# Layer 1 of a two-layer model: the last 52 of 128 slot scatters made in the experts' stage, row loads that wait by expert

## The chip, the cores and the metric

The kernel runs on one core of a Trainium2 chip. The metric is the time of one execution on the device in microseconds (us), lower is better. Before the change three runs took 2988.72, 2998.57 and 2993.95 us, median 2993.95. Engines: PE (TensorE), DVE (VectorE), ACT (ScalarE), POOL (GpSimd) and SP (SyncE), which mostly issues DMAs. DMAs issued by SP go over queue q1, those of ACT over q10, those of POOL (the indirect ones) over q0. They share 16 DMA engines.

## The reference

x is (4, 512, 512) in float32, 2048 tokens of 512 numbers. Four steps are added to it one after the other: a state-space layer, a first mixture of experts, a cross attention and a second mixture of experts. The change touches only the second mixture ("layer 1"):

```python
scores = sigmoid(x @ router_w)                      # 2048 tokens x 32 experts
# the best 4 of 8 groups of experts, then the best 8 experts of those (with a bias)
tkw = 2.5 * scores[chosen] / sum(scores[chosen])
xs = repeat(x, 8)[sort by expert]                   # 16384 rows, sorted by expert
down = (silu(xs @ w_gate[e]) * (xs @ w_up[e])) @ w_down[e]
routed = sum over a token's 8 rows of down * tkw
out = x + routed + silu(x @ sw_gate) * (x @ sw_up) @ sw_down     # x normalised in each
```

Each expert has w_gate and w_up of 512 x 256 and w_down of 256 x 512.

## The kernel before

Each stage is a block with a program for every engine; a barrier of all engines stands between two stages. Two stages make up layer 1.

**The routing stage** (`route_stage` with L = 1). DVE normalises the tokens into the tile `xn` (r_xn in the trace), PE and ACT make the logits, and DVE picks 8 experts for each token. Every expert gets a run of slots in the DRAM tensor `slots_in1`, in half tiles of 64 slots. A token's 8 slots stand in `scat`, the largest first (DVE's MAX8 gives them in falling order), so k = 7 is the slot of its lowest expert. POOL then copies the rows into their slots with 128 indirect DMAs (line 882, "scatters"): one for each of 16 tiles of 128 tokens and each k. Four semaphores `written` count them in turn. In the first half scatter n waits until n-2 has landed, in the second half until n-4 has. Beside this PE computes the shared expert (lines 1218 and 1237), and DVE adds it to x (line 1046). SP loads the weights of the first three experts and stores x to the output. The stage ends with waits for all 128 scatters and for all stores.

**The experts' stage** (`expert_stage1`). It walks over 144 tiles of 128 slots. ACT loads the rows in groups of four tiles into a ring of two groups (line 1933 the rows in four pieces, 1938 and 1940 the weights and token numbers), and reloads a ring place while the tiles pass (`reload`, called in turn t). For each tile PE does gate and up (2092), turns the hidden rows (2101) and does down (2114), in the order turn(t-1), up(t), down(t-1). DVE transposes rows (2009), copies the turned hidden rows (2014), multiplies (2019), finds each row's weight and address (`addressed`, 2038 to 2045) and copies half of w_down (2027). ACT makes silu (1921), scales the result into one of `OUT` = 8 result tiles `yo` (1928), and copies half of the gate and up weights (1947). POOL adds each result tile to the output with two indirect DMAs of 64 rows (1874, "adds"), so there are 288 of them. SP refills the weights of an expert when `down` of the last tile of an earlier one is done.

The ring of eight result tiles ties POOL to the others. `added` is raised when POOL starts the adds of tile t (from t = 2 on), which means that tile t-2 has landed. Before the address and the result of tile t are written, for t from 8 on, DVE (`addressed`) and ACT (`empty`) wait until tile t-8 has landed, that is until POOL starts the adds of tile t-6. In DVE's order `addressed(t)` stands ahead of the copy of the weights for tile t+1 and of the hidden rows of tile t.

Of the kernel before, what the change touches and what calls it, by code (L numbers as in the profile page):

```python
# [48 lines left out]
AHEAD = RING1 - 1  # L49
XW = H + 32  # L50
# [28 lines left out]
class Pools:  # L79
# [15 lines left out]
    def sem0(self, name):  # L95
        self.from0.append(self.sem(name))
        return self.from0[-1]

# [597 lines left out]

def route_stage(nc, c, I, D, x, L, route, ahead=None, out=None):
# [10 lines left out]
    with ExitStack() as ctx:  # L708
# [7 lines left out]
        if L == 0:  # L716
            xn, xnT = route["xn"], route["xnT"]
        else:
            xn = sb("xn", [P, NT, XW])
            xnT = sb("xnT", [P, B, KH, S])  # L720
# [60 lines left out]
        NARROW = NT * K if L == 0 else NT * K // 2  # L781
        written = [pl.sem0(R + f"written{lane}") for lane in range(LANES)]
# [6 lines left out]
        with nc.Block() as block:  # L789

            @block.sync
            def _(sp):
# [46 lines left out]
                else:  # L839
                    for a in range(2):  # L840
                        sp.dma_start(out[T + a * P:T + (a + 1) * P, :].rearrange("p (a z) -> p a z", z=P),
                                     bc(c["zeros"][:, :], 1, H // P)).then_inc(sem["xout"], 16)
# [4 lines left out]
                    for b in range(B):  # L847
                        sp.wait_ge(sem["xadd"], 1 + TB * (b + 1))
                        sp.dma_start(out[b * S:(b + 1) * S, :].rearrange("(t p) h -> p t h", p=P),
                                     x[:, b * TB:(b + 1) * TB, :]).then_inc(sem["xout"], 16)  # L850
                    sp.wait_ge(sem["eidout"], 1 + 16)
                    sp.wait_ge(sem["ahead"], 1 + 48 * AHEAD)
                    sp.wait_ge(sem["xout"], 1 + 16 * (B + 2))

            @block.gpsimd
            def _(pool):
# [14 lines left out]
                for t in range(NT):  # L871
                    if L == 1 and t < TB:
                        pool.wait_ge(sem["idx0"], 1 + t + 1)
                    else:
                        pool.wait_ge(sem["idx"], 1 + t // TB + 1 - L)
                    for k in range(K):
                        n = t * K + k
                        lane = n % LANES
                        ahead_of = n - 2 if n < NARROW else n - LANES
                        if ahead_of >= 0:  # L880
                            pool.wait_ge(written[ahead_of % LANES], 16 * (ahead_of // LANES + 1))
                        pool.indirect_dma_start(slots[:, :], bass.IndirectOffsetOnAxis(scat[:, t, k:k + 1], 0),  # L882
                                                xn[:, t, 0:XU], None, bounds_check=nslot - 1, oob_is_err=False)\
                            .then_inc(written[lane], 16)
                for lane in range(LANES):
                    pool.wait_ge(written[lane], 16 * NT * K // LANES)
# [52 lines left out]
            def _(dve):  # L939
# [188 lines left out]
                if L == 1:  # L1128
# [8 lines left out]
                    dve.tensor_copy(tei[:, :], te[:, :]).then_inc(sem["eid"], 1)  # L1137
                if L == 0:
# [640 lines left out]
def expert_stage1(nc, c, I, D, x, ends, W, out):  # L1779
# [3 lines left out]
    with ExitStack() as ctx:  # L1783
# [4 lines left out]
        OUT = 2 * RING  # L1788
        assert E % RING == 0
        assert AHEAD == RING - 1  # L1790
        wgu, wd = W["wgu"], W["wd"]
        assert OUT == 2 * RING
# [47 lines left out]
        with nc.Block() as block:  # L1840

            @block.sync
            def _(sp):
# [22 lines left out]
            def _(pool):  # L1866
# [3 lines left out]
                pool.iota(within_i[:, :], [[32, NTILE1 // 2], [0, 2]], base=0, channel_multiplier=0).then_inc(sem["iota"], 1)  # L1870
                pool.wait_ge(sem["after"], 1 + 2)
# [45 lines left out]
            def _(act):  # L1917
# [31 lines left out]

                def reload(t, q):  # L1950
                    place = q % RING
                    if place == RING - 2:
                        hold(act, sem["xsT"], 1 + t + 2, c["held"])
                        load_rows((t + RING + 2) * P, q // RING, (0, 1))
                    if place == RING - 1:
                        load_rows((t + RING + 1) * P, q // RING, (2,))
                    if place == 0:
                        load_rows((t + RING) * P, 1 - q // RING, (3,))
                    if place == 1:
                        hold(act, sem["dest"], 1 + t - 1, c["held"])  # L1960
                        load_rec((t + RING - 1) * P, 1 - q // RING)
# [29 lines left out]
                for q in range(REST):  # L1991
                    t = (TURNS - 1) * OUT + q
                    gate(t, q)
                    if q < 2:
                        reload(t, q)
# [6 lines left out]
            def _(dve):  # L2002
# [27 lines left out]
                def addressed(t, q, n):  # L2030
                    row = rec[:, q // RING, q % RING, :]
                    word = token[:, q // RING, q % RING * 2:q % RING * 2 + 2, 0]
                    if q % RING == 0:
                        dve.wait_ge(rec_in[q // RING], 32 * n)
# [13 lines left out]
                def a_round(i, first=False, last=False):  # L2048
                    for q in range(REST if last else OUT):
                        t = i * OUT + q  # L2050
                        if not (last and q == REST - 1):
                            turned_rows(t + 1, q + 1, i + (q + 1) // OUT + 1)
# [3 lines left out]
                        addressed(t, q, i + 1)  # L2056
# [1067 lines left out]
def program(nc, I, out, upto=9):  # L3124
    with ExitStack() as ctx:
# [34 lines left out]
        if upto >= 5:  # L3160
            route1 = {"ln": ln1, "wr": wr1, "bias": bias1, "scat": pl.sb("scat1", [P, NT, K1], I32), "ends": pl.sb("ends", [1, 1 + E], I32)}
            W = {"wgu": pl.sb("e1_wgu", [P, RING1, KH, 2 * F1]), "wd": pl.sb("e1_wd", [P, RING1, F1 // P, H])}
            route_stage(nc, c, I, D, x, 1, route1, W, out)
        if upto >= 6:
            expert_stage1(nc, c, I, D, x, route1["ends"], W, out)
# [52 lines left out]
```

## Time and profile before

| | |
|---|---|
| median of three runs | 2993.95 us |
| the profiled execution | 2994.6 us |
| its span in the profile | 2992.8 us |
| PE busy | 2622.1 us (88%) |
| DVE busy | 1535.3 us (51%) |
| ACT busy | 1032.8 us (35%) |
| POOL busy | 1294.2 us (43%) |

How to read it: a share is that of the whole span, over stages with different limits. Layer 1 lies in the last third. The chain that ended last is followed back from the last instruction. In a timeline row the number in square brackets is how long the engine stood idle before the instruction, and the name behind the arrow is what ended this; "issue" means nothing that the profile shows.

### The profile page before, as it was taken

Reading aid. Unit: us, or ns where it says so; the run is one execution under the profiler, and the core shown is the slowest. Engines: PE = TensorE matmul, PEld = TensorE weight load, DVE = VectorE, ACT = ScalarE, POOL = GpSimd, SP = SyncE. Lnnn points to the kernel's source line nnn. Section 1 sums busy time; section 2 is a strip of 40 time slices with the busy share of each in tenths; the row PEclk is TensorE's granted clock in tenths of the full one; section 3 lists DMA queues with packets and bytes.
Section 4 is the critical chain, followed back from the end, with each engine's and each line's share of the span. In section 5 each row is a group of like instructions: output and inputs, shape, how many; then the busy total and the mean of one; then the engine's idle time right before and its main releaser. Section 6 shows DMA issues by size and latency. Waiting matters only on the chain. (4 is left out here: it accounts for less than half of the span.)

```text
span 2992.8 us, 41291 instructions
## 1 busy us (share of the span) xinstructions
PE 2622.1 (88%) x11315; PEld 1086.1 (36%) x11318; DVE 1535.3 (51%) x2654; ACT 1032.8 (35%) x1305; POOL 1294.2 (43%) x933
## 2 busy tenths in 40 slices
PE   5888976699999987768999999798099999999998
PEld 1343432244444433323333333443033333333333
DVE  7999999631110032136666564731045555555554
ACT  4646564120000011023443333200055555555553
POOL 2767656312300032116565633146535455545554
PEclk8999999999999999889999999899599999999999
DMA  3433222310210289982067100254657776787764
GB/s 127 116 96 105 86 64 71 123 50 22 86 33 14 80 283 353 287 216 82 1 175 195 42 1 1 73 217 187 207 137 158 160 155 121 139 219 158 161 119 61
DMA packets 361887, 372.82 MB, mean 125 GB/s; under 512 B 85810, under 2 KB 268403, under 8 KB 361778
## 3 DMA queue, kind: packets, MB, share of 16 engines
q1 hardware_dynamic: 202210, 239.03, 25.4%
q0 software_dynamic: 45520, 93.26, 14.7%
q10 hardware_dynamic: 114048, 39.16, 5.9%
q8 instruction: 58, 0.95, 0.1%
q14 instruction: 51, 0.42, 0.1%
HBM read 231.96 MB, written 152.14 MB: 128 GB/s over the span
## 5 line engine op out<-in xcount | busy, mean ns | idle before, releaser
L1874 POOL DMA_INDIRECT out_x<-e_yo,e_dest x288 | 418.7, 1454 | 411.0 <-DMA out_x<-e_yo,e_dest 281.4
L2092 PE MATMUL e_psg<-e_wgu,e_xsT 128*64 x1152 | 519.9, 594 | 83.0 <-ACT e_cgu L1947 83.0
L2092 PE MATMUL e_psg<-e_cgu,e_xsT 128*64 128x512 f32 x1152 | 519.9, 594 | 0.0
L287 POOL TENSOR_TENSOR hc<-hs,bcst 128x1024 f32<-128x1024 f32 x128 | 300.8, 2350 | 179.6 <-DVE ps_b L507 170.6
L1947 ACT ACTIVATE e_cgu<-e_wgu 128x2048 f32 x144 | 275.1, 1911 | 133.0 <-issue 130.6
L632 PE MATMUL ps_y<-hc,ident 128*128 128x512 f32 x512 | 241.2, 609 | 89.4 <-POOL hc L287 89.2
L513 DVE TENSOR_TENSOR_SCAN hs<-dA,ps_b 128x1024 f32<-128x1024 f32 x128 | 292.7, 2286 | 8.1 <-ACT dA L417 3.9
L2092 PEld LDWEIGHTS e_psg<-e_wgu,e_xsT 128*64 128x64 f32 x1152 | 154.2, 137 | 332.0 <-issue 332.0
L2114 PE MATMUL e_pso<-e_wd,e_hT 128*64 x576 | 270.7, 592 | 0.7 <-DVE e_hT L2014 0.7
L2114 PE MATMUL e_pso<-e_cd,e_hT 128*64 128x512 f32 x576 | 270.7, 592 | 0.0
L1237 PE MATMUL r_ps_t<-r_wd,r_h 128*128 128x512 f32 x480 | 210.7, 600 | 9.6 <-DVE r_h L984 5.1
L917 ACT ACTIVATE r_sg<-r_ps_g 128x512 f32<-128x512 f32 x60 | 35.8, 597 | 525.2 <-PE r_ps_g L1218 493.8
L984 DVE TENSOR_TENSOR r_h<-r_ps_u,r_sg 128x512 f32<-128x512 f32 x60 | 41.4, 692 | 319.3 <-PE r_ps_u L1218 289.8
L417 ACT ACTIVATE dA<-dt,a_neg 128x511 f32<-128x511 f32 x256 | 165.2, 713 | 102.4 <-DVE hs L513 97.4
L2702 DVE TENSOR_REDUCE a_nm<-a_ps 128x2 f32<-128x992 f32 x128 | 146.1, 1185 | 89.5 <-PE a_ps L2946 89.1
L2019 DVE TENSOR_TENSOR e_h<-e_psg,e_sg 128x256 f32<-128x256 f32 x144 | 61.2, 425 | 254.0 <-ACT e_sg L1921 232.2
L2464 ACT ACTIVATE a_pt<-a_ps 128x1024 f32<-128x1024 f32 (+1 forms) x128 | 126.2, 1022 | 181.0 <-PE a_ps L2963 120.2
L882 POOL DMA_INDIRECT slots_in<-r_xn,scat x128 | 126.3, 987 | 133.9 <-DMA slots_in<-r_xn,scat 54.6
L632 PEld LDWEIGHTS ps_y<-hc,ident 128*128 128x128 f32 x512 | 92.8, 191 | 232.4 <-POOL hc L287 138.5
L2009 DVE STREAM_TRANSPOSE e_xsT<-e_xs 128x512 f32<-128x512 f32 x144 | 168.4, 1169 | 5.5 <-DMA e_xs<-slots_in 5.5
L1928 ACT ACTIVATE e_yo<-e_pso,e_wrow 128x512 f32<-128x512 f32 x144 | 99.1, 688 | 207.7 <-PE e_pso L2114 178.5
L2027 DVE COPY e_cd<-e_wd 128x1024 f32 x144 | 101.9, 708 | 129.4 <-PE e_pso L2114 113.0
(426 smaller groups left out, 4202.3 us busy)
## 6 DMA issues: line engine op xcount, KB each, us to landing
slots_in<-zeros SPq DMA_DIRECT2D x144, 256.0 KB
e_xs<-slots_in ACTq DMA_DIRECT2D x144, 256.0 KB
bcst<-bc_rows SPq DMA_DIRECT2D x128, 256.0 KB, 4.2
e_wgu<-in_wg SPq DMA_DIRECT2D x32, 512.0 KB
e_wgu<-in_wu SPq DMA_DIRECT2D x32, 512.0 KB
e_wd<-in_wd SPq DMA_DIRECT2D x32, 512.0 KB
e_w<-in_wg SPq DMA_DIRECT2D x11, 1408.0 KB
e_w<-in_wu SPq DMA_DIRECT2D x11, 1408.0 KB
```

The lines of the kernel that those rows point to most:

```text
L287: pool.tensor_tensor(hc[:, it % 2, half(h), :], hs[:, it % 2, half(h), :], bc(bcst[:, q, 1, :], 1, HB), ALU.mult).then_inc(sem["hc"], 1)
L417: i = act.activation(dA[:, it % 2, t, 1:], dt[:, b % 2, t, 1:], ACT.Exp, scale=a_neg[:, n, t:t + 1])
L513: dve.tensor_tensor_scan(hs[:, it % 2, half(h), :].rearrange(flat), dA[:, it % 2, half(h), :].rearrange(flat), ps_b[:, :, :].rearrange(fla ...
L632: i = pe.matmul(ps_y[:, t, :], c["ident"][:, :], hc[:, it % 2, t, :], start=False, stop=False, skip_group_check=True)
L882: pool.indirect_dma_start(slots[:, :], bass.IndirectOffsetOnAxis(scat[:, t, k:k + 1], 0), xn[:, t, 0:XU], None, bounds_check=nslot - 1, oo ...
L1237: i = pe.matmul(ps_t[:, j % 2, :], h[:, f, j * P:(j + 1) * P], wd[:, f, :], start=f == 0, stop=f == FC - 1)
L1874: pool.indirect_dma_start(out[:, :], bass.IndirectOffsetOnAxis(dest[:, q, s:s + 1], 0), yo[half(s), q, :], None, bounds_check=T + 2 * P - ...
L1947: act.activation(cgu[:, q % 2, :, :], wgu[:, bass.ds(e % RING, 1), :, :].rearrange("p o k n -> p (o k) n"), ACT.Copy).then_inc(sem["cgu"], 1)
L2009: dve.transpose(xsT[:, q % 2, :, :].rearrange("p k (s j) -> p k s j", j=DQ), xs[:, q // RING % 2, part, :].rearrange("p s (i k) -> p k s i ...
L2092: j = pe.matmul(ps_g[half(s), q % 2, :], xsT[:, q % 2, k, half(s)], w, start=k == 0, stop=k == KH - 1, tile_position=(0, s * HALF), skip_g ...
L2114: j = pe.matmul(ps_o[half(s), q % 2, :], hT[:, q % 2, a, half(s)], w, start=a == 0, stop=a == NW - 1, tile_position=(0, s * HALF), skip_gr ...
L2702: dve.tensor_reduce(nm[:, i % 8, 2 * z:2 * z + 2], ps[:, at:at + 2, 0:S2], AX_X, ALU.max, negate=True)\
```

## The change

POOL makes 76 scatters in the routing stage and the other 52 in the experts' stage, ahead of its first add. The order is new: `SLOT_ORDER` has the 32 of tokens 0 to 511 as before, then for tokens 512 and on by rank, k = 7 of all twelve tiles of tokens, then k = 6, and so on. Every scatter now waits for n-2. The wait for all 128 and for the stores of x stands ahead of POOL's first add. The tile `xn` and the semaphores live across both stages.

ACT loads a group of rows when the scatters that can write to it have landed. DVE works this out in the routing stage for groups 0 to 3, by the experts that end ahead of the group's last half tile (ten small instructions, `rows_held`). ACT reads the number, and waits on the four semaphores. It now loads group 1 behind the first two copies of weights. SP makes its first refill of weights only when group 1 has landed. No load beyond the last group is made any more. `OUT` is 8 as before; the rest of the edits (`PER`, `% 2`, `GROUPS`) write the same numbers in a general form.

```diff
+LANES1 = 4
+SLOT_ORDER = [(t, k) for t in range(TB) for k in range(K1)] + [(t, k) for k in reversed(range(K1)) for t in range(TB, NT)]
+EARLY = 76
+GROUPS_HELD = 4
...
+def write_slots(pool, D, route, n):
+
+    t, k = SLOT_ORDER[n]
+    written = route["written"]
+    if n >= 2:
+        pool.wait_ge(written[(n - 2) % LANES1], 16 * ((n - 2) // LANES1 + 1))
+    pool.indirect_dma_start(D["xs1"][:, :], bass.IndirectOffsetOnAxis(route["scat"][:, t, k:k + 1], 0),
+                            route["xn"][:, t, 0:H + 2 * K1 + 1], None, bounds_check=NSLOT1 - 1, oob_is_err=False)\
+        .then_inc(written[n % LANES1], 16)
...
-                    sp.wait_ge(sem["xout"], 1 + 16 * (B + 2))
...
+                    for n in range(EARLY):
+                        if n < TB * K and n % K == 0:
+                            pool.wait_ge(sem["idx0"], 1 + n // K + 1)
+                        if n == TB * K:
+                            pool.wait_ge(sem["idx"], 1 + B - 1)
+                        write_slots(pool, D, route, n)
...
+                    for g in range(GROUPS_HELD):
+                        step(dve.tensor_scalar(past[0:1, :], tcum[0:1, :], float(2 * RING1 * (g + 1) - 1), None, ALU.is_le))
+                        step(dve.tensor_reduce(tf[0:1, g:g + 1], past[0:1, :], AX_X, ALU.add))
+                    held = tf[0:1, 0:GROUPS_HELD]
+                    per_rank = 16 * TB * (B - 1) // LANES1
+                    step(dve.tensor_scalar(held, held, float(K1 - 1), None, ALU.min))
+                    step(dve.tensor_scalar(route["rows_held"][:, :], held, float(per_rank), float(16 * TB * K1 // LANES1 + per_rank),
+                                           ALU.mult, ALU.add), wait=False)
...
                 for s in range(AHEAD):
                     announce(s, 0)
+                sp.wait_ge(rows_in[1], 16 * NQ)
...
+                for n in range(EARLY, len(SLOT_ORDER)):
+                    write_slots(pool, D, route, n)
+                for lane in range(LANES1):
+                    pool.wait_ge(written[lane], 16 * NT * K1 // LANES1)
+                pool.wait_ge(stored, 16 * (B + 2))
                 pool.wait_ge(sem["after"], 1 + 2)
...
+                def rows_written(g):
+                    if isinstance(g, int) and g < GROUPS_HELD:
+                        count = act.value_load(route["rows_held"][0:1, g:g + 1], min_val=16, max_val=16 * NT * K1 // LANES1)
+                        for lane in range(LANES1):
+                            hold(act, written[lane], count, c["held"])
...
-                for r in range(2):
-                    load_rows(r * RING * P, r)
-                    load_rec(r * RING * P, r)
+                rows_written(0)
+                load_rows(0, 0)
+                load_rec(0, 0)
                 act.wait_ge(sem["ids"], 1 + 16)
                 copied(0, 0)
                 copied(1, 1)
+                rows_written(1)
+                load_rows(RING * P, 1)
+                load_rec(RING * P, 1)
```

POOL at the border of the two stages, before (slots_in<-r_xn,scat are the scatters, out_x<-e_yo,e_dest the adds, the branches the border):

```order
L866 IOTA r_token_i 128x16
L882 DMA slots_in<-r_xn,scat 18432x544 x128
L789 UNCONDITIONAL_BRANCH
L108 ISA
L1865 UNCONDITIONAL_BRANCH
L1867 IOTA e_sloti 128x144
L1868 IOTA e_sparei 128x4
L1869 IOTA e_afteri 1x288
L1870 IOTA e_withini 1x144
L1874 DMA out_x<-e_yo,e_dest 2304x512 x6
```

And POOL at the same place in the changed kernel (line 711 is the scatter, 1911 the add):

```order
L883 IOTA r_token_i 128x16
L711 DMA slots_in<-r_xn,scat 18432x544 x76
L807 UNCONDITIONAL_BRANCH
L116 ISA
L1897 UNCONDITIONAL_BRANCH
L1899 IOTA e_sloti 128x144
L1900 IOTA e_sparei 128x4
L1901 IOTA e_afteri 1x288
L1902 IOTA e_withini 1x144
L711 DMA slots_in<-r_xn,scat 18432x544 x52
L1911 DMA out_x<-e_yo,e_dest 2304x512 x6
```

52 scatters have moved from ahead of the barrier to behind it, and they stand ahead of every add.

DVE in the routing stage in the changed kernel, from the table of experts to the next product of the shared expert (r_h); before, r_h followed directly on r_tei:

```order
L1155 TENSOR_SCALAR ends<-r_ti 1x32
L1156 TENSOR_SCALAR r_te<-r_te 128x3
L1157 CAST r_tei<-r_te 128x3
L1159 TENSOR_SCALAR r_past<-r_tcum 1x32
L1160 TENSOR_REDUCE r_tf<-r_past 1x1
...
L1163 TENSOR_SCALAR r_tf<-r_tf 1x4
L1164 TENSOR_SCALAR rows_held<-r_tf 1x4
L1004 TENSOR_TENSOR r_h<-r_ps_u,r_sg 128x512 x2
```

The pair of lines 1159 and 1160 stands there four times, so ten instructions are new ahead of the two products.

## Rows read from the trace of the kernel before

**Rows 1.** Timeline of PE at the border (start, us, engine, line, tiles, idle before)

```profile
2073.57 14.00 PE L1237 MATMUL r_ps_t<-r_wd,r_h 128*128 128x512 f32 x32 [0.85 <-DVE r_h L984]
...
2170.53 1.11 PE L2092 MATMUL e_psg<-e_wgu,e_xsT 128*64 x1 [82.96 <-ACT e_cgu L1947]
```

**Rows 2.** Busy time by stretch (us, PE, PEld, DVE, ACT, POOL, clock, DMA share, GB/s)

```profile
2087.00:2171.00 84.00, 1.04 (x4) 0.30 (x4) 5.46 (x10) 2.70 (x2) 46.07 (x49) 0.53 0.62 205
...
2215.00:2300.00 85.00, 85.00 (x488) 32.86 (x486) 45.41 (x125) 44.96 (x46) 51.97 (x35) 1.00 0.75 154
```

**Rows 3.** Timeline of POOL at the border

```profile
2146.71 0.98 POOL L882 DMA_INDIRECT slots_in<-r_xn,scat  x1 [0.31 <-issue]
2153.37 0.24 POOL L1867 IOTA e_sloti<- 128x144 int32 x1 [5.68 <-POOLq L104]
...
2155.11 0.47 POOL L1870 IOTA e_withini<- 1x144 int32 x1
```

**Rows 4.** Timeline of DVE, the small instructions in the routing stage

```profile
1940.34 0.23 DVE L1131 TENSOR_SCALAR r_past<-r_tcum,tile_no 128x32 f32<-128x32 f32 x1
...
1940.83 0.24 DVE L1131 TENSOR_SCALAR r_past<-r_tcum,tile_no 128x32 f32<-128x32 f32 x1
...
1942.60 1.29 DVE L984 TENSOR_TENSOR r_h<-r_ps_u,r_sg 128x512 f32<-128x512 f32 x2
```

**Rows 5.** Timeline of PE, down of the shared expert behind it

```profile
1943.99 16.62 PE L1237 MATMUL r_ps_t<-r_wd,r_h 128*128 128x512 f32 x32 [3.56 <-issue]
```

**Rows 6.** Timeline of POOL, two scatters of one parity with no other traffic

```profile
2030.69 0.98 POOL L882 DMA_INDIRECT slots_in<-r_xn,scat  x1 [1.26 <-DMA slots_in<-r_xn,scat]
...
2034.23 0.98 POOL L882 DMA_INDIRECT slots_in<-r_xn,scat  x1 [1.20 <-DMA slots_in<-r_xn,scat]
```

**Rows 7.** Timeline of POOL, scatters 5 and 13, weights of three experts loading between

```profile
1942.40 0.98 POOL L882 DMA_INDIRECT slots_in<-r_xn,scat  x1 [0.85 <-DMA slots_in<-r_xn,scat]
...
1967.92 0.98 POOL L882 DMA_INDIRECT slots_in<-r_xn,scat  x1 [2.12 <-DMA slots_in<-r_xn,scat]
```

**Rows 8.** DMA queues from 2300 to 2500 us (packets, MB, share of 16 engines)

```profile
q10 hardware_dynamic: 28501, 9.79, 21.8%
q1 hardware_dynamic: 8400, 11.01, 17.0%
...
e_wd<-in_wd SPq DMA_DIRECT2D x7, 512.0 KB
```

**Rows 9.** Timeline of SP, last load of the refill that follows tile 9

```profile
2234.86 0.57 SPq L1775 DMA_DIRECT2D e_wd<-in_wd  x1
```

**Rows 10.** Timeline of POOL, adds of tiles 0 (both), 1 (second), 2 and 3 (first)

```profile
2184.57 1.51 POOL L1874 DMA_INDIRECT out_x<-e_yo,e_dest  x1 [28.99 <-ACT e_yo L1928]
2189.14 1.80 POOL L1874 DMA_INDIRECT out_x<-e_yo,e_dest  x1 [3.06 <-DMA out_x<-e_yo,e_dest]
...
2202.76 1.41 POOL L1874 DMA_INDIRECT out_x<-e_yo,e_dest  x1 [2.98 <-DMA out_x<-e_yo,e_dest]
2207.67 1.42 POOL L1874 DMA_INDIRECT out_x<-e_yo,e_dest  x1 [3.49 <-DMA out_x<-e_yo,e_dest]
...
2216.66 1.42 POOL L1874 DMA_INDIRECT out_x<-e_yo,e_dest  x1 [0.32 <-issue]
```

**Rows 11.** Timeline of DVE, `addressed` and the hidden copy of tiles 8 and 7

```profile
2221.20 0.23 DVE L2038 SCALAR_TENSOR_TENSOR e_mine<-e_rec,e_slot 128x8 f32<-128x8 f32 x1
...
2224.38 0.38 DVE L2014 COPY e_hT<-e_psh 128x256 f32<-128x256 f32 x1
```

**Rows 12.** Timeline of PE, down of tile 8

```profile
2225.74 0.59 PE L2114 MATMUL e_pso<-e_wd,e_hT 128*64 x1
```

**Rows 13.** Chain that ended last, from 2160 to 2190 us (start, us, what)

```profile
2170.53 5.68 PE e_psg L2092 x16
...
2177.79 3.43 PE e_psg L2092 x16
```

**Rows 14.** Timeline of DVE, the last add of the shared expert

```profile
2119.47 0.69 DVE L1046 TENSOR_TENSOR x_resid<-r_ps_t,x_resid 128x512 f32<-128x512 f32 x1 [21.71 <-remote]
```

More of the change, by code:

```diff
@@ L780, in route_stage @@
         LANES = 4
-        NARROW = NT * K if L == 0 else NT * K // 2
-        written = [pl.sem0(R + f"written{lane}") for lane in range(LANES)]
+        written = [pl.sem0(R + f"written{lane}") for lane in range(LANES)] if L == 0 else route["written"]
         tiled = "(k p) n -> p k n"
@@ L869, in _ @@
                     pool.tensor_tensor(rs[:, b % 2, :], ve[:, b % 2, :], c["minus_half"][:, 0:TB], ALU.pow).then_inc(sem["rs"], 1)
[L871 to L886, printed above, removed]
+                if L == 0:
+                    for t in range(NT):
+                        pool.wait_ge(sem["idx"], 1 + t // TB + 1)
+                        for k in range(K):
+                            n = t * K + k
+                            if n >= 2:
+                                pool.wait_ge(written[(n - 2) % LANES], 16 * ((n - 2) // LANES + 1))
+                            pool.indirect_dma_start(slots[:, :], bass.IndirectOffsetOnAxis(scat[:, t, k:k + 1], 0),
+                                                    xn[:, t, 0:XU], None, bounds_check=nslot - 1, oob_is_err=False)\
+                                .then_inc(written[n % LANES], 16)
+                    for lane in range(LANES):
+                        pool.wait_ge(written[lane], 16 * NT * K // LANES)
+                else:
+                    for n in range(EARLY):
[4 more added lines that the diff above has]
+                        write_slots(pool, D, route, n)
             @block.scalar
@@ L1776, in expert_weights, with expert_stage1 @@
                  .rearrange("o (p c) n -> p (o c) n", c=F1 // P)).then_inc(sem, 16)
-def expert_stage1(nc, c, I, D, x, ends, W, out):
+def expert_stage1(nc, c, I, D, x, route, W, out):
     with ExitStack() as ctx:
@@ L1788, in expert_stage1 @@
         OUT = 2 * RING
+        PER = OUT // (2 * RING)
+        ends, written, stored = route["ends"], route["written"], route["stored"]
+        pl.adopt(written + [stored])
         assert E % RING == 0
@@ L1791, in expert_stage1 @@
         wgu, wd = W["wgu"], W["wd"]
-        assert OUT == 2 * RING
+        assert OUT == 2 * RING * PER and GROUPS_HELD * RING == OUT + 2 * RING
         GROUPS = -(-NTILE1 // RING)
@@ L2055, in a_round @@
                         product(t, q)
-                        addressed(t, q, i + 1)
+                        addressed(t, q, i * PER + q // (2 * RING) + 1)
                         if not (last and q == REST - 1):
@@ L3160, in program @@
         if upto >= 5:
-            route1 = {"ln": ln1, "wr": wr1, "bias": bias1, "scat": pl.sb("scat1", [P, NT, K1], I32), "ends": pl.sb("ends", [1, 1 + E], I32)}
+            route1 = {"ln": ln1, "wr": wr1, "bias": bias1, "scat": pl.sb("scat1", [P, NT, K1], I32), "ends": pl.sb("ends", [1, 1 + E], I32),
+                      "xn": pl.sb("r1_xn", [P, NT, H + 2 * K1 + 2]), "rows_held": pl.sb("rows_held", [1, GROUPS_HELD], I32),
+                      "written": [pl.sem(f"r1_written{lane}") for lane in range(LANES1)], "stored": pl.sem("r1_stored")}
             W = {"wgu": pl.sb("e1_wgu", [P, RING1, KH, 2 * F1]), "wd": pl.sb("e1_wd", [P, RING1, F1 // P, H])}
@@ L3164, in program @@
         if upto >= 6:
-            expert_stage1(nc, c, I, D, x, route1["ends"], W, out)
+            expert_stage1(nc, c, I, D, x, route1, W, out)
             return
```

42 lines of the change are left out of this document (24 added, 18 removed).

## The prediction

> **What bounds the kernel now.** I read the chain that ended last first. In the last third it runs over PE alone, tile after tile of the experts' stage, so that stage is bound by PE from its first matmul to its end: 85.00 of 85.00 us busy, at a granted clock of 1.00 [rows 2]. What can be won lies ahead of its first matmul. PE ends the shared expert at 2087.57 (2073.57 + 14.00) and starts the experts at 2170.53, behind 82.96 us of idle time [rows 1]. The timeline of POOL shows why: the last scatter starts at 2146.71, and the next stage begins at 2153.37 [rows 3]. In that stretch POOL is the one busy engine, 46 of 84 us [rows 2]. So the change moves the right thing. The question is who waits for the moved scatters next, and that is the ring of eight result tiles: POOL can't add a tile before the last slot is written, PE can't get more than about eight tiles ahead of the adds. So I time one event in both kernels, the start of the adds of tile 2, which frees the ring for tile 8. Before, it is at 2207.67 [rows 10], and DVE asks for it only at 2221.20, in `addressed` of tile 8 [rows 11]: 13.5 us of slack.
>
> **The start of the stage.** DVE gets ten small instructions ahead of the product that PE waits for. A pair takes 0.49 us (1940.34 to 1940.83), the last two some 0.2 each: 4 x 0.49 + 0.4 = 2.35 us. The products follow at 1942.60 and end at 1943.89 [rows 4], and PE starts at 1943.99 behind 3.56 us idle [rows 5]. So this is on the path, since PE has no other idle stretch up to the border. The last product of the stage then ends at 2087.57 + 2.35 = 2089.9, DVE's add 0.7 later (its duration in [rows 14]), at 2090.6. From the last scatter to the next stage are 6.66 us (2146.71 to 2153.37) [rows 3]. Of these 3.54 are its landing and POOL's waking (below), 3.1 the border. With 0.8 for the store that SP still issues the new stage begins at 2094.5, against 2153.37: 58.9 us earlier. POOL's 76 scatters are no obstacle: the one at 2034.23 [rows 6] is number 49, counted from 0, and 26 more at the pitch below start by 2080.3.
>
> **The moved scatters.** Without other traffic two scatters of one parity start 3.54 us apart (2030.69, 2034.23) [rows 6]: landing plus waking, two in flight, 1.77 us each. After the iotas (2153.37 to 2155.58 [rows 3]), 2.2 us, and 0.3 of issue the first starts at 2097.0, the last 51 x 1.77 = 90.3 us later, and it has landed and woken POOL after 3.54: 2190.8. That is X = 0, no contention.
>
> X, the cost of the other queues, I take from the one stretch where scatters run beside loads of weights. From scatter 5 at 1942.40 to scatter 13 at 1967.92 are 25.5 us, and 8 x 1.77 are 14.2 [rows 7]: 11.4 us more for three experts, 3.8 us each. In the experts' stage four experts' weights load before POOL is through: the first refill, and those behind tiles 1, 4 and 9, the last of which ends its issue at 2234.86, 81.5 us into the stage [rows 9]. 4 x 3.8 = 15.2 us. The row loads of groups 0 to 3 pass too. Beside these no scatter runs in the trace, so I bound them. A group costs the engines 21.8% of 200 us for nine groups, 4.8 us; an expert 17.0% of 200 for seven, 4.9 us [rows 8]. So a group costs at most what an expert does: 4 x 3.8 = 15.2. From below it is nothing: two steps of the adds that wait for a landing take 4.57 us (tile 0) and 4.91 (tile 1 to 2) [rows 10], 0.3 apart, though ACT reloads rows all through the stage. I take 2 us each, nearer the adds, 8 us. POOL issues beside a busy DVE: adds take 1.41 to 1.80 us [rows 10], and 52 scatters at 0 to 0.2 more are 0 to 10 us; I take 2, as only landings are waited for. X = 15 + 8 + 2 = 25 us, between 15 (weights alone) and 42. A gain below nothing is excluded: each wait is for a landing, and more traffic makes none earlier. POOL's first add then starts at 2215.8.
>
> **The ring.** From the first add to that of tile 2 are four steps, each one a landing. They take 23.1 us before (2184.57 to 2207.67), with two bursts of weights in them; a step without one is 4.57 us (2184.57 to 2189.14) [rows 10]. PE stands by then, so no refill is running: 18 us, 2233.8. (Before's 23 is the upper end.) DVE wanted this at 2221.20: 12.6 us late.
>
> What comes after it: before, down of tile 8 starts at 2225.74 [rows 12], 4.5 us behind `addressed`. On restart the copy of weights, the transpose and the hidden copy follow at once, some 3.6 us, so 0.9 is won back. PE starts cold again: its first tile takes 5.68 us where the next takes 3.43 [rows 13], so 2.25 are lost. Net +1.4. The adds of tile 3 come 9 us after those of tile 2 before (2207.67, 2216.66) [rows 10], and their turn at DVE 5.6 later; without the burst they come 6 later, which the shorter restart covers. From there POOL is faster than PE (adds 1.7 to 2 us apart, two per tile of 5.59), and the rest of the stage runs as before, 14.0 us later.
>
> Other edits: the row loads need 56, 68, 80 and 92 scatters. Experts 0, 1 and 2 end with tiles 1, 4 and 9 by SP's refills, which gives these numbers. The first two are done by the border, the other two 4 and 16 scatters later, ahead of turns 2 and 6. They cost nothing, and if they did, it would be hidden behind the ring. Loading group 1 behind the first copies of weights can only let PE start sooner, and that is lost at the ring as well. Where the early start goes: before, PE starts 17.2 us into the stage (2153.37 to 2170.53), so now by 2112 at the latest. It does tiles 0 to 9 by about 2165 (5.59 us each) and then stands for some 70 us.
>
> **Sum.** 2994.6 (the profiled execution) + 14.0 = 3008.6. The median of the runs shown is 0.65 lower: **3008 us**.
>
> **Rivals.**
> *The queues share evenly (X = 10).* By the trace, a scatter beside weights has a pitch of 25.5 / 8 = 3.2 us [rows 7]; if only its own transfer were doubled, a pitch of about 2.1 would do. With X = 10 the sum is 3008 - 15 = 2993, no change. For it: the three experts of [rows 7] came in one burst, in the stage they come one by one, with SP waiting between. Against it: even 2.1 us beside four groups and four experts, some 39 us of engine time, gives about 10, and the one row there is says more.
> The Trainium skill, "DMA: Bandwidth & Descriptors", section "Queues, rings and completion order", says that each DMA engine goes round-robin between its queue rows packet by packet. 
> *The moved scatters are done in time (faster).* X near 0 gives 3008 - 25 = 2983. It decides from X under 2 us on. For it: POOL's steady pitch of 1.77 is latency, and the DMA engines are at 0.75 in the stage. Against: [rows 7]. Were the ring not to bind at all, it would be 2994 - 59 = 2935; I give that 2 in 100.
> *Rows cost what weights do, and DVE holds POOL up (much slower).* X = 42, and 23 us to tile 2: 3008 + 17 + 5 = 3030. For it: rows come in many small packets, 28501 for 9.79 MB [rows 8].
> *DVE's last adds are held up again.* Before, the last one comes 21.7 us late while POOL issues without a pause [rows 14], unseen. If that stays, the border comes some 20 us later and the ring with it: 3028. Against: POOL is through with its 76 before DVE gets there.
> *The change does nothing new to the ring.* It doesn't: `OUT` was eight, and so the ring's slack is the old one. That is in the forecast.
>
> **Chances.** The forecast 0.42 (3000 to 3018), even sharing 0.24 (2986 to 3000), in time 0.14, much slower 0.17, held-up adds 0.03. A measurement can tell some 0.3% from no change, 9 us. Faster by more 0.14; within 0.24; slower 0.62. The range 2986 to 3030 leaves out the cases in time and the outermost of the slow ones. The forecast's own range is 3000 to 3018.
>
> **What would show it.** In the profile after: the experts' stage begins at about 2094, PE's idle stretch ahead of it shrinks from 83 to about 20 us, and a second one of some 70 us stands behind tile 9, released through DVE from an add on POOL. POOL's 52 scatters stand in the new stage with a mean pitch near 2.2 us (1.77 + 25/52); the first add starts near 2216, tile 2's near 2234. The last tile ends 14 us later than before. I am wrong if the scatters' pitch is under 2.0 (then X is under 12), if PE has no second gap, or if the adds come at more than 5.6 us a tile after the restart, so that PE stops again.

## The result and the profile after

The kernel after took 3008.25 us, median of 5 runs (3005.17 to 3013.44), against 2993.95 for the kernel before (5 runs, 2988.72 to 2998.57): a ratio of 1.0048, interval 1.0036 to 1.006. The prediction was 3008. The profiled execution has a span of 3008.0 us, against 2992.8: 15.2 us more.

POOL at the border, from the timeline (start, duration, engine and line, operation, tile written <- tiles read, idle time before it and what ended it):

```profile
2083.83 0.98 POOL L711 DMA_INDIRECT slots_in<-r_xn,scat  x1 [0.41 <-issue]
2092.97 0.24 POOL L1899 IOTA e_sloti<- 128x144 int32 x1 [8.16 <-POOLq L112]
2095.35 1.01 POOL L711 DMA_INDIRECT slots_in<-r_xn,scat  x1 [0.18 <-issue]
2096.67 0.98 POOL L711 DMA_INDIRECT slots_in<-r_xn,scat  x1 [0.30 <-issue]
2102.22 0.98 POOL L711 DMA_INDIRECT slots_in<-r_xn,scat  x1 [4.57 <-DMA slots_in<-r_xn,scat]
...
2147.54 0.98 POOL L711 DMA_INDIRECT slots_in<-r_xn,scat  x1 [5.15 <-DMA slots_in<-r_xn,scat]
...
2213.34 0.98 POOL L711 DMA_INDIRECT slots_in<-r_xn,scat  x1 [1.02 <-DMA slots_in<-r_xn,scat]
2217.13 1.50 POOL L1911 DMA_INDIRECT out_x<-e_yo,e_dest  x1 [2.81 <-issue]
2221.78 1.44 POOL L1911 DMA_INDIRECT out_x<-e_yo,e_dest  x1 [3.15 <-DMA out_x<-e_yo,e_dest]
...
2235.45 1.62 POOL L1911 DMA_INDIRECT out_x<-e_yo,e_dest  x1 [3.23 <-DMA out_x<-e_yo,e_dest]
```

The stage begins at 2092.97, 60.4 us ahead of [rows 3]. The 52 moved scatters run from 2095.35 to 2213.34: 118.0 us for 51 steps, a pitch of 2.31. The adds of tile 0 begin at 2217.13 and those of tile 2, which free the ring for tile 8, at 2235.45 (before: 2207.67, [rows 10]). The pitch is a mean of two stretches. Up to 2164.96, about as long as PE works and rows and weights load, 24 steps take 69.6 us, 2.90 each; the last 27, with PE standing at the ring and nothing else loading, take 48.4 us, 1.79 each.

PE and DVE at the places of [rows 1, 11, 12, 14], from their timelines:

```profile
2074.93 14.00 PE L1265 MATMUL r_ps_t<-r_wd,r_h 128*128 128x512 f32 x32 [0.85 <-DVE r_h L1004]
2103.63 1.11 PE L2141 MATMUL e_psg<-e_wgu,e_xsT 128*64 x1 [14.70 <-DVE e_xsT L2058]
2238.49 1.11 PE L2163 MATMUL e_pso<-e_wd,e_hT 128*64 x1 [76.80 <-DVE e_hT L2063]
```

```profile
2088.96 0.69 DVE L1066 TENSOR_TENSOR x_resid<-r_ps_t,x_resid 128x512 f32<-128x512 f32 x1 [2.74 <-PE r_ps_t L1265]
2234.87 0.23 DVE L2087 SCALAR_TENSOR_TENSOR e_mine<-e_rec,e_slot 128x8 f32<-128x8 f32 x1 [77.86 <-POOLq L1932]
...
2237.92 0.38 DVE L2063 COPY e_hT<-e_psh 128x256 f32<-128x256 f32 x1
```

The one idle stretch of 82.96 us has become two: 14.70 ahead of the stage's first matmul and 76.80 ahead of the down matmuls of tile 8. The second ends through DVE, whose `e_mine` of tile 8 stood 77.86 us until POOL counted the adds of tile 2. Tile 8's down matmuls start at 2238.49, 12.75 us behind [rows 12].

The chain of waits at the restart (start, duration, what):

```profile
2238.49 3.68 PE e_pso L2163 x8
2242.17 0.85 PE e_psh L2150 x8
2243.03 3.55 PE e_psg L2141 x16
2246.58 1.72 PE e_pso L2163 x8
...
2252.16 1.72 PE e_pso L2163 x8
```

The first tile takes 8.09 us (2238.49 to 2246.58) where the next ones take 5.59: 2.5 us for the lower clock at the restart (granted clock 0.50 from 2238 to 2243, 0.98 from 2243 to 2247). 12.75 + 2.5 = 15.25, the whole difference of the spans. That the two traces can be compared like this is owed to their earlier stages, which no edit touches: the last instruction of POOL ahead of the scatters (IOTA of `r_token_i`) starts at 1887.16 before and at 1887.39 after. The stretches of the stage (time, busy us and instructions of the engines, granted clock, DMA share, GB/s):

```profile
2104.00:2161.00 57.00, 53.05 (x294) 19.88 (x292) 25.36 (x67) 25.81 (x26) 19.56 (x19) 0.98 0.79 226
2162.00:2238.00 76.00, 0.00 (x0) 0.00 (x0) 2.20 (x7) 0.13 (x1) 35.94 (x35) 0.52 0.35 115
2239.00:2324.00 85.00, 85.00 (x478) 32.51 (x476) 44.72 (x119) 44.34 (x44) 51.35 (x35) 0.98 0.78 157
```

PE works through tiles 0 to 7, stands for 76 us at the lower clock (0.52, the 1.2 GHz level), and from then on is as busy as in [rows 2].

### The profile page after: what moved, and what is told of

The parts are those of the page before. It is cut to its first block and busy times, and to the rows that moved or that the text cites. A ratio compares the mean times of both kernels' runs of the same rounds, so it can differ in the third digit from the quotient of the medians.

```text
span 3008.0 us, 41320 instructions
## 1 busy us (share of the span) xinstructions
PE 2622.9 (87%) x11317; PEld 1082.7 (36%) x11318; DVE 1540.9 (51%) x2664; ACT 1032.0 (34%) x1305; POOL 1294.5 (43%) x933
## 5 line engine op out<-in xcount | busy, mean ns | idle before, releaser
L2141 PE MATMUL e_psg<-e_wgu,e_xsT 128*64 x1152 | 519.5, 594 | 14.7 <-DVE e_xsT L2058 14.7
L1984 ACT ACTIVATE e_cgu<-e_wgu 128x2048 f32 x144 | 275.2, 1912 | 65.6 <-issue 64.2
```

The source lines that it names most:

```text
L1984: act.activation(cgu[:, q % 2, :, :], wgu[:, bass.ds(e % RING, 1), :, :].rearrange("p o k n -> p (o k) n"), ACT.Copy).then_inc(sem["cgu"], 1)
L2141: j = pe.matmul(ps_g[half(s), q % 2, :], xsT[:, q % 2, k, half(s)], w, start=k == 0, stop=k == KH - 1, tile_position=(0, s * HALF), skip_g ...
```

## The experiments

Each is compared with the kernel before, run on the same chip (2994 to 2995 us, 9 to 13 runs). Scatters are counted from 0; 76 to 127 are the moved ones. The stages ahead of layer 1 end up to 12 us apart from trace to trace, though no experiment touches them (that IOTA starts at 1882.3 in the earliest, at 1894.4 in the latest). So absolute times of two traces can't be set against each other to a microsecond. Where it matters, the time of layer 1 alone is given, from that IOTA to the end of the span: 1105.6 us before, 1120.6 after.

**ring16: sixteen result tiles.**

```diff
-GROUPS_HELD = 4
+GROUPS_HELD = 6
-        OUT = 2 * RING
+        OUT = 4 * RING
```

> The changed kernel with a ring of 16 result tiles in place of 8, nothing else. Theory (POOL's backlog is the bound, the ring only says when PE meets it): in the changed kernel the adds of tile 10 start 42.3 us after those of tile 2 (2277.72 and 2235.45), and PE takes 44.7 us for eight tiles, so a ring of 16 wins about 2 us: 3006 us, 3002 to 3008. PE's second gap moves from tile 9 to tile 17 and shrinks to about 35 us. Rival (the ring is too small): PE gets eight tiles further before it stops and keeps them, 44.7 us less, 2964 us.

With a deeper ring PE reaches the row loads of groups 4 and 5 before the scatters are done, so these need a hold too; that is the edit of `GROUPS_HELD`.

Measured: 2981.18 us (2974.57 to 2986.41, 6 runs), ratio 0.9958 (0.9941 to 0.9974), near neither number. I had misread the ring: tile t waits for the adds of tile t - OUT + 2, so with sixteen, tile 16 waits for those of tile 2, the same event as tile 8 before. From POOL's timeline, and from PE's list of waits (us in total, times, longest):

```profile
2229.40 0.98 POOL L711 DMA_INDIRECT slots_in<-r_xn,scat  x1 [0.81 <-DMA slots_in<-r_xn,scat]
2233.20 1.50 POOL L1911 DMA_INDIRECT out_x<-e_yo,e_dest  x1 [2.82 <-issue]
...
2251.39 1.64 POOL L1911 DMA_INDIRECT out_x<-e_yo,e_dest  x1 [3.20 <-DMA out_x<-e_yo,e_dest]
```

```profile
PE e_pso L2163 <- DVE e_hT L2063: 30.0, 1, 30.0
PE e_psg L2141 <- DVE e_xsT L2058: 14.3, 1, 14.3
```

The gap moved from tile 8 to tile 16 and shrank from 76.8 to 30.0 us, as PE did eight tiles more (44.7 us) ahead of it. So the ring is what the moved scatters hit. Since PE works on, more rows and weights are loaded beside the scatters, whose pitch rises from 2.31 to 2.59 (2097.59 to 2229.40), and the event itself comes 16 us later. Between the results of tiles 7 and 15 some 13 us more go (58.0 us instead of 44.7): ACT holds the row loads of groups 4 and 5 until the scatters that they need have landed, 4.8 us (2172.06 to 2176.90) and 9.1 us (2198.72 to 2207.80).

**ahead4: the moved scatters four in flight.**

```diff
+    back = 2 if n < EARLY else LANES1
-        pool.wait_ge(written[(n - 2) % LANES1], 16 * ((n - 2) // LANES1 + 1))
+        pool.wait_ge(written[(n - back) % LANES1], 16 * ((n - back) // LANES1 + 1))
```

> The changed kernel, but each of the 52 moved scatters waits for the one four ahead of it instead of two. Theory (the moved scatters are bound by the latency of two in flight, longer beside other queues): with four in flight the mean pitch falls from 2.31 us to 1.3 to 1.5, the last scatter comes 42 to 50 us earlier, and so do the adds and PE's restart: 2958 to 2970 us. Rival (the other queues take bandwidth, not latency): the contention X of 28 us stays, only the pitch without it falls from 1.77 to 1.29, 25 us: 2983 us. Rival (other waits bind behind them): no change, 3008.

Measured: 2973.58 us (2970.59 to 2976.89, 4 runs), ratio 0.993 (0.9913 to 0.9946). From POOL's timeline:

```profile
2178.01 0.98 POOL L712 DMA_INDIRECT slots_in<-r_xn,scat  x1 [0.30 <-issue]
2179.29 0.98 POOL L712 DMA_INDIRECT slots_in<-r_xn,scat  x1 [0.30 <-issue]
2180.58 0.98 POOL L712 DMA_INDIRECT slots_in<-r_xn,scat  x1 [0.30 <-issue]
2184.88 1.50 POOL L1912 DMA_INDIRECT out_x<-e_yo,e_dest  x1 [3.32 <-issue]
...
2203.32 1.62 POOL L1912 DMA_INDIRECT out_x<-e_yo,e_dest  x1 [3.29 <-DMA out_x<-e_yo,e_dest]
```

51 steps take 84.1 us (pitch 1.65) instead of 118.0, the adds of tile 2 start 32 us earlier, PE's gap is 43.1 us, and 34.7 us are gained. The theory is right in kind and a little too bold: it had a pitch of 1.3 to 1.5 and 2958 to 2970 us. Both rivals (2983 and 3008) fell. The diff had a part that I had not priced as such: in the kernel before, scatters 0 to 63 wait for n-2 and 64 to 127 for n-4; after, all wait for n-2. The move and the loss of depth are two changes.

**all_early and all_early4: nothing moved, with the waits of after and with those of before.**

```diff
-EARLY = 76
+EARLY = 128
```

all_early4 has this and in `write_slots`:

```diff
+    back = 2 if n < 64 else LANES1
-        pool.wait_ge(written[(n - 2) % LANES1], 16 * ((n - 2) // LANES1 + 1))
+        pool.wait_ge(written[(n - back) % LANES1], 16 * ((n - back) // LANES1 + 1))
```

> The changed kernel with all 128 scatters in the routing stage (EARLY = 128), still two in flight, order and waits as changed. Theory: the routing stage ends with POOL, 52 x 1.77 = 92 us after 2083.8, so the experts' stage begins at about 2182.6 instead of 2153.4 before; PE starts 10.7 us into it instead of 17.2, and there is no second gap: 2993.95 + 29 - 6.5 = 3016 us. So the move itself would be worth 8 us, and waiting for n-2 in the second half cost 25. Rival (the move itself costs, the waits don't): 2994 or less. DVE's last two adds of the shared expert come without the stalls of the kernel before if these come from scatters issued without a pause.

> All 128 scatters ahead of the border, as before the change, and with its waits too: scatters 0 to 63 wait for n-2, 64 to 127 for n-4. What is left of the change are the ten instructions on DVE and the new order of row loads. Theory (the change took the second half's depth away together with the move; depth is worth 0.52 us a scatter from 76 on, 26.5 us, and 6 us on 64 to 75): 3019.0 - 32.5 = 2986 to 2989, under the time before the change by the earlier first matmul (10.7 instead of 17.2 us into the stage) less 1.4 us for the ten instructions. DVE's last two adds are held up again (over 10 us idle each). Rival (depth matters only beside other traffic): under 10 us gained, 3009 to 3019.

Measured: all_early 3019.01 us (3016.1 to 3028.81, 4 runs), ratio 1.0081 (1.0064 to 1.0099). all_early4 2989.71 us (2983.42 to 2998.2, 10 runs), ratio 0.9985 (0.9975 to 0.9996). Both came out near their theories. Depth alone is worth 29.3 us when nothing is moved (33.2 in layer 1 of the two traces, 1132.6 and 1099.4): a pitch of 1.87 against 1.34 for scatters 76 to 127. At a depth of two, moving the scatters gains 10.8 us (3019.0 to 3008.25); at four, 16.1 (2989.7 to 2973.6). By layer 1 of the traces the two gains are 12.0 and 12.6 us, so the difference between them is not shown. So the move is worth having at either depth. The change was slower than before because it took the depth away with it.

The rest of the change gains a little by itself: all_early4 is 4.4 us under the kernel before. Its PE starts 10.6 us into the experts' stage (2149.19 to 2159.82) where before it took 17.2, with group 1 loaded behind the first copies of weights. So the way from before to after is some 4 us won by the other edits, 29 lost by the depth, and 11 won by the move.

The same pair shows what holds DVE up. DVE's last adds of the shared expert, first in all_early, then in all_early4, and a row of POOL in each just then:

```profile
2092.35 0.69 DVE L1066 TENSOR_TENSOR x_resid<-r_ps_t,x_resid 128x512 f32<-128x512 f32 x1 [2.74 <-PE r_ps_t L1265]
2095.78 0.69 DVE L1066 TENSOR_TENSOR x_resid<-r_ps_t,x_resid 128x512 f32<-128x512 f32 x1 [2.74 <-PE r_ps_t L1265]
2096.17 0.98 POOL L711 DMA_INDIRECT slots_in<-r_xn,scat  x1 [1.18 <-DMA slots_in<-r_xn,scat]
```

```profile
2088.18 0.98 POOL L712 DMA_INDIRECT slots_in<-r_xn,scat  x1 [0.30 <-issue]
2089.47 0.98 POOL L712 DMA_INDIRECT slots_in<-r_xn,scat  x1 [0.30 <-issue]
...
2092.48 0.69 DVE L1067 TENSOR_TENSOR x_resid<-r_ps_t,x_resid 128x512 f32<-128x512 f32 x1 [14.77 <-remote]
2114.18 0.69 DVE L1067 TENSOR_TENSOR x_resid<-r_ps_t,x_resid 128x512 f32<-128x512 f32 x1 [21.01 <-issue]
```

With two in flight POOL pauses 1.18 us at every second scatter, and DVE adds at PE's pace. With four it does not pause there (0.30), and the same two adds stand 14.77 and 21.01 us, as in [rows 14]. It costs nothing there, since POOL is later still.

**all_early_ring16: all_early and ring16 together.** (Both edits are shown above.) The theory was that the ring is free in time once the slots are written ahead of the border, so that sixteen tiles change nothing against all_early, 3019 us give or take 3; the rival was a difference of over 5 us, because the ring costs something throughout the stage.

Measured: 3024.65 us (3020.57 to 3031.02, 4 runs), ratio 1.011 (1.0088 to 1.0132). The median is 5.6 us over all_early, outside the theory's range, but the intervals of the two ratios overlap, and layer 1 takes 1132.6 us in the trace of all_early and 1132.9 in this one. So the ring costs nothing while the scatters stay ahead of the border, and the 27 us that ring16 gained belong to the moved scatters.

**late_refills: SP loads no further expert until all slots are written.**

```diff
                 sp.wait_ge(rows_in[1], 16 * NQ)
+                for lane in range(LANES1):
+                    sp.wait_ge(written[lane], 16 * NT * K1 // LANES1)
```

> The changed kernel, but SP makes its first refill of weights only when all 128 scatters have landed. Theory (weights are 15 of the 28 us of contention, 3.8 an expert): the last scatter comes 15 us earlier, and the time falls by 10 to 15 us, since expert 3 is wanted just behind the restart: 2993 to 2999 us. Rival (the row loads are nearly all of the contention): no gain, 3008, or more if PE waits for expert 3.

Measured: 3003.45 us (3001.49 to 3009.65, 7 runs), ratio 1.0033 (1.0016 to 1.005). From POOL's timeline:

```profile
2199.91 0.98 POOL L711 DMA_INDIRECT slots_in<-r_xn,scat  x1 [0.99 <-DMA slots_in<-r_xn,scat]
2203.70 1.50 POOL L1913 DMA_INDIRECT out_x<-e_yo,e_dest  x1 [2.81 <-issue]
...
2228.23 1.62 POOL L1913 DMA_INDIRECT out_x<-e_yo,e_dest  x1 [4.63 <-DMA out_x<-e_yo,e_dest]
```

The scatters take 109.1 us (2090.80 to 2199.91), 8.9 less than in the kernel after, so three experts' weights cost 8.9 us there, one trace set against one. What is left over 90.3 is 18.8 us, with the row loads as the one other data traffic in the stretch (a few packets of instruction loads apart). No run takes the row loads away, so that the 18.8 are theirs is by elimination. The refills then ran beside the adds: tile 0 to tile 2 took 24.5 us instead of 18.3. So 6.2 of the 8.9 were given back, and neither my theory nor the rival of no gain was met in full. The medians differ by 4.8 us, layer 1 of the two traces by 3.2.

**all_three: ahead4 and ring16 together.** (The scatters four in flight, sixteen result tiles; both edits are shown above.)

> The changed kernel with the moved scatters four in flight (n waits for n-4 from 76 on) and a ring of sixteen result tiles. Theory (the adds' ring is what the moved scatters hit; with both changes it is late for nothing): adds of tile 2 at about 2203 to 2209, and tile 16 wants its place at about 2204 (yo(8) would stand at 2166 without the stall, and eight tiles of 5.59 us later is 2211, 6.7 us behind the adds). So of the 43.1 us gap that the kernel with four in flight still has, at most 5 us stay: 2973.6 - 44 + 0 to 5 = 2930 to 2935, PE without a stretch of over 8 us idle behind the first matmul of the stage. Rival (rows and not results hold PE: ACT waits for scatters ahead of the row loads of groups 4 and 5, as tiles 9 to 15 lost 13 us in the kernel with sixteen alone): 2940 to 2950, with idle stretches of PE of 5 to 13 us around tiles 9 to 15 whose releaser is ACT.

Measured: 2950.89 us (2947.04 to 2963.36, 4 runs), ratio 0.9871 (0.9843 to 0.9898). It beats both kernels, by 43 and 57 us, but is 16 to 21 us over the theory. The ring hardly binds: the adds of tile 2 start at 2201.32, tile 16's result comes at 2224.98, 5.59 behind that of tile 15. The loss lies ahead of it: tiles 7 to 15 took 60.2 us instead of 44.7. ACT's timeline there, and POOL's (the four scatters shown are the last of 16 that stand 1.28 to 1.29 us apart, from 2155.98 on but for one of 1.54):

```profile
2159.24 0.69 ACT L1966 ACTIVATE e_yo<-e_pso,e_wrow 128x512 f32<-128x512 f32 x1 [1.33 <-issue]
2160.34 1.92 ACT L1985 ACTIVATE e_cgu<-e_wgu 128x2048 f32 x1 [0.41 <-issue]
2168.79 0.38 ACT L1959 ACTIVATE e_sg<-e_psg 128x256 f32<-128x256 f32 x1 [6.54 <-remote]
2178.69 0.69 ACT L1966 ACTIVATE e_yo<-e_pso,e_wrow 128x512 f32<-128x512 f32 x1 [9.51 <-DMA bcst<-bc_rows]
```

```profile
2171.65 0.98 POOL L712 DMA_INDIRECT slots_in<-r_xn,scat  x1 [0.30 <-issue]
2172.94 0.98 POOL L712 DMA_INDIRECT slots_in<-r_xn,scat  x1 [0.30 <-issue]
2174.23 0.98 POOL L712 DMA_INDIRECT slots_in<-r_xn,scat  x1 [0.30 <-issue]
2175.51 0.98 POOL L712 DMA_INDIRECT slots_in<-r_xn,scat  x1 [0.30 <-issue]
2179.30 1.62 POOL L1912 DMA_INDIRECT out_x<-e_yo,e_dest  x1 [2.81 <-issue]
```

Tile 8's result had its address from DVE since 2158.6 and its sum from PE since 2165, and the gate of tile 9 its sums since 2163. ACT did the one at 2168.79 and the other at 2178.69, 3.2 us behind the start of the last scatter. The tile that the profile names as releaser (`bcst`) belongs to an earlier stage, so the name says nothing. The rival had foreseen ACT idle there, but for the row loads' waits, and these are not it: at tile 10 the row load is issued 0.2 us behind the gate (2181.34, 2181.53).

**three_80: four in flight from 64 on, and 80 scatters ahead of the border.** The diff is against all_three.

```diff
-EARLY = 76
+EARLY = 80
-    back = 2 if n < EARLY else LANES1
+    back = 2 if n < 64 else LANES1
```

> As the one before it, but four in flight from scatter 64 on (as in the kernel before the change) and 80 scatters instead of 76 ahead of the border. Theory (POOL is through with the 80 before DVE's last add, since scatters 64 to 79 take 1.35 us each: the 80th starts at about 2084; and the ring is no longer what binds): the border stays at 2093, the time equals that of the one before within 4 us. Rival (unpaused scatters beside DVE hold up DVE's last adds, as in the kernel before the change, 15.5 and 21.7 us): the border comes 5 to 20 us later, and the kernel is 5 to 20 us slower than the one before it; DVE's last add then has over 5 us idle ahead of it.

Measured: 2951.83 us (2946.41 to 2954.62, 4 runs), ratio 0.9854 (0.9835 to 0.9873): the time of all_three within 1 us, as the theory says. DVE's last add has 1.69 us idle ahead of it, the one before it 3.55, so the rival fell. The experts' stage begins at 2100.49 in this trace, 7 us behind the theory, but so much later is its routing stage too: from the IOTA on it is 207.0 us against 206.7 in all_three.

**three_pause and three_deep3: all_three with pauses, and with three in flight.**

```diff
-    back = 2 if n < EARLY else LANES1
+    back = 2 if n < EARLY or n % 8 == 0 else LANES1    # three_pause
+    back = 2 if n < EARLY else 3                       # three_deep3
```

> The kernel with sixteen result tiles and four scatters in flight, but every eighth of the moved scatters (80, 88, ... 120) waits for n-2 instead of n-4, so that POOL pauses there. Theory (a long row of scatters 0.30 us apart holds ACT and DVE up until POOL pauses: in the kernel without these pauses scatters 108 to 127 stood like that from 2156 to 2176, and the result of tile 8 came at 2178.69 instead of some 2165, which with a smaller loss behind it is 15 us between tiles 7 and 15): each pause costs POOL about 1 us, 6 in all, the adds of tile 2 come at about 2207; tile 8's result comes by 2168; of the 15 us lost between tiles 7 and 15 about 10 are won back, and the ring takes 0 to 3. 2950.9 - 10 = 2941 (2937 to 2945). Rival (ACT and DVE wait there for something else, row loads or weights behind full DMA engines): tile 8's result stays at 2175 or later, and the time at 2949 to 2957.

> The kernel with sixteen result tiles, but three scatters in flight (n waits for n-3) behind the border instead of four. Landing and waking take 3.54 us, so three in flight could start every 1.18 us, under the 1.28 us that POOL takes for one: without traffic there is no pause either. Theory (it is the pause that counts, and three in flight leave few of them): ACT and DVE are held up in the last twenty scatters nearly as with four, tile 8's result comes at 2173 or later, the mean pitch is 1.65 to 1.9, and the time 2949 to 2957. Rival (one scatter fewer in the queues lets the other loads through): pitch 1.8 or more, no idle stretch of ACT over 5 us, and 2938 to 2946.

Measured: three_pause 2952.49 us (2945.0 to 2958.78, 5 runs), ratio 0.9852 (0.9832 to 0.9872); three_deep3 2954.46 us (2950.63 to 2955.59, 4 runs), ratio 0.9863 (0.9845 to 0.988). No gain from the pauses: a miss. ACT in three_pause, from its timeline:

```profile
2165.59 0.69 ACT L1966 ACTIVATE e_yo<-e_pso,e_wrow 128x512 f32<-128x512 f32 x1 [1.33 <-issue]
2174.06 0.38 ACT L1959 ACTIVATE e_sg<-e_psg 128x256 f32<-128x256 f32 x1 [5.45 <-remote]
...
2233.46 0.69 ACT L1966 ACTIVATE e_yo<-e_pso,e_wrow 128x512 f32<-128x512 f32 x1 [14.15 <-PE e_pso L2164]
```

Tile 8's result came at 2165.59, as the theory asked, and tiles 7 to 15 took 55.1 us, 5 less. But six pauses cost the scatters 15.9 us (100.05 instead of 84.16 for 51 steps), not 6; the adds of tile 2 start at 2226.68, and tile 16 stands at the ring (14.15). The rival's time (2949 to 2957) came, but not its sign, a result of tile 8 at 2175 or later. With three in flight tile 8's result came at 2162.86 (the theory had 2173 or later), tile 9's only at 2180.17 behind idle stretches of 7.17 and 6.72 us; the pitch of 1.97 is over the range of the theory, the time within it. All four kernels of this family end within 4 us. In three_pause and three_deep3 the ring takes what the engines win: tile 16's result stands 14.15 us in the one and 9.90 in the other.

## Why the prediction was right, step by step

**The start of the stage.** The ten instructions were priced at 2.35 us and cost 2.2: PE stands 5.78 us ahead of the product at 1946.42, where it stood 3.56 [rows 5]. But PE ended the shared expert at 2088.93, only 1.36 us behind before, because those 32 matmuls then took 15.54 us instead of 16.62, which the prediction did not foresee. The border (2092.97) came 1.5 us ahead of the forecast of 2094.5. DVE's last adds kept PE's pace, so the rival of the held-up adds fell. The reason given against it, that POOL is through by then, was true (2083.83 against 2088.96) but not needed: in all_early POOL still scatters, two in flight, and the adds keep PE's pace all the same. It is the depth that counts.

**The moved scatters.** Two in flight at 1.77 us, plus X. X is 118.0 - 90.3 = 27.7 us; the forecast was 25. The first add started at 2217.13, forecast 2215.8: the 2.7 us more of X are partly made up by a first scatter that came 1.65 us early (2095.35, forecast 2097.0). The mechanism held, but the terms inside X were mis-sized and cancelled, so that X came out this close was luck. Weights: 15.2 forecast, 8.9 measured. I had counted four experts; only three fell in the stretch, since the refill behind tile 9 can't start while PE stands at tile 8 (SP's timeline, here the loads of the down weights):

```profile
2111.85 0.67 SPq L1803 DMA_DIRECT2D e_wd<-in_wd  x1
...
2122.68 0.57 SPq L1803 DMA_DIRECT2D e_wd<-in_wd  x1
...
2139.45 0.57 SPq L1803 DMA_DIRECT2D e_wd<-in_wd  x1
...
2249.93 0.57 SPq L1803 DMA_DIRECT2D e_wd<-in_wd  x1
```

And each cost 3.0 us, not 3.8. Rows, with POOL's own slowing: 10 forecast, 18.8 measured. "2 each, nearer the adds" was the wrong choice between the bounds; four groups at 4.7 are above even the upper one of 3.8. POOL's own slowing is small in this: the issues of the 52 scatters are together 1.0 us longer than 0.98 each, against the 2 us put down for it. Steps of the adds were no measure for what rows cost a scatter. It is not that they had met none: ACT's queue (q10) took 17.9% of the engines in the step of 4.57 us, with rows, and 14.9% in that of 4.91, mostly with the small records of weights and tokens [rows 10]. With nothing beside them such steps take 4.42 to 4.65 us in the kernel after. So ACT's loads cost an add nearly nothing there and a scatter much; why is open. Beside weights the adds do slow down (24.5 against 18.3 us in late_refills).

**Even sharing** (X = 10, 2993 us) fell. The Trainium skill, "DMA: Bandwidth & Descriptors", section "Queues, rings and completion order", has each engine take packets from its queue rows in turn. That a scatter would then lose no more than its own transfer time was my reading of it, since the rule counts packets and not time. The reading does not hold here: POOL stood up to 5.15 us between two scatters (2147.54), and the pitch beside the loads was 2.90, where the prediction gave 2.1 to even sharing. X = 0 and X = 42 fell with the same number.

**The ring.** Adds of tile 0 to tile 2: 18.3 us, forecast 18. DVE's `addressed` of tile 8 came 13.7 us behind [rows 11] (forecast 12.6), down of tile 8 12.75 later (11.7), the cold restart 2.5 (2.25). Sum 15.25, forecast 14.0. The idle stretches came as foretold, 14.70 us (about 20) and 76.80 (some 70), the second ahead of the down matmuls of tile 8 with gate and up of tile 9 done, and PE did not stop again but for 0.7 us once. ring16 shows by an experiment that the ring is the bound: with eight tiles more, the gap comes eight tiles later.

**The row loads' waits** were priced at nothing. ACT did stand for group 3 (`e_yo` at 2148.50 behind 6.37 us idle), which the ring's gap swallowed, as the prediction allowed. In ring16, where the gap is smaller, such waits cost some 13 us.

**Not priced apart.** The forecast used the right pitch for two in flight, but never said that before had four in flight for these scatters. Whoever asks why the change is slower finds the answer there and not in the contention: X at a depth of four is still 18.5 us over 65.6, and the kernel is 20 us faster than before.

**Open.** Why an engine stands beside a long row of unpaused scatters. It is shown that DVE's adds stand 14.8 and 21.0 us at four in flight and not at two, with nothing else changed. In the experts' stage holds of ACT go together with such rows (17.75 us in ahead4, ending at 2180.96, 0.4 us behind the start of the last scatter; 9.51 in all_three), but in three_deep3 one ends inside a row (2173.06). DMA engines that are full are not the reason in the routing stage: from 2077.7 to 2114.9 of all_early4, over both stalls, only the scatters' queue moves data, at 54.6% of the engines, and no instruction load shows. In ahead4, over the 17.75 us, it is 54.8%, with one packet of instructions beside it. Whether it is POOL's writing of descriptors or something else was not separated.

## What to carry to other kernels

When work is moved behind a border, ask which ring or counter it now stands ahead of, and time the one event that frees it in both kernels; that event, with the chain behind it, gave the result here to 1 us, with the help of errors that cancelled. Read from the diff also what the moved instructions wait for: the depth of two instead of four cost more than the move won. And when a bound is taken away, price what the engine set free will load meanwhile: sixteen result tiles let PE do 44.7 us more of work ahead of its gap and made the scatters 13.8 us slower.

## What the runs showed of the hardware

- Indirect scatters with two in flight start every 1.77 us without other traffic, with four every 1.28 to 1.29 us, which is POOL's own 0.98 + 0.30. Behind the border the means over 51 steps are 2.31 and 1.65; the steps beside loads alone, with two in flight, are 2.90.
- Row loads in small packets seem to slow the scatters more for their engine time than weights do: 18.8 us for 22.5 us of engine time (11570 packets, 4.29 MB, in the 109.1 us of late_refills), against 8.9 for 14.7 (3600 packets, 4.72 MB, in the 118 us of the kernel after). Both figures come from the difference of two traces, and the 18.8 hold whatever else slows a scatter there.
- One pause in a row of four in flight cost some 2.6 us (15.9 / 6, from one trace each, other traffic's share of it not told apart), not the 1 us that had been put down for it.
